# Edge items of a graph layer: ScalarE writes the gathered rows of x into the bank that the last layer adds to, and the sorting net's transpose stands last in its step

## The reference, cut to what matters

```
# x: (50000, 128)  src, dst: (12500,), dst sorted  edge_attr: (12500, 128)
edge_sum = segment_sum(edge_attr, src, num_segments=50000)
h   = elu(concatenate([x, edge_sum], axis=1) @ W0 + b0)
h   = elu(h @ W2 + b2)
out = layernorm(x + h @ W3 + b3)          # over the 128 features
```

## Time and profile before

| | |
|---|---|
| median of 3 runs | 547.99 us (544.12 to 551.29) |
| profiled execution | 546.7 us, of which span 544.9 us |
| PE busy | 507.9 us, 93% of the span |
| DVE busy | 459.7 us, 84% |
| ACT busy | 418.9 us, 77% |
| POOL busy | 371.8 us, 68% |
| mean granted TensorE clock | 0.986 of full speed |
| moved by DMA | 96.98 MB, mean 178 GB/s |

### The profile page before, as it was taken

How to read it: one execution, slowest core, us unless ns; L and a number is a source line. 1 busy time by engine, 2 the same in 40 slices (tenths; PEclk the granted TensorE clock), 3 DMA queues, 4 the chain that set the end, 5 groups by cost and what they waited for, 6 DMA issues and landing times.

```text
span 544.9 us, 10037 instructions
## 1 busy us (share of the span) xinstructions
PE 507.9 (93%) x2881; PEld 362.2 (66%) x2881; DVE 459.7 (84%) x1216; ACT 418.9 (77%) x1534; POOL 371.8 (68%) x311
## 2 busy tenths in 40 slices
PE   6898999879979999999999999999999999999980
PEld 4465656556656767777777777777777777777670
DVE  7999888878989988898898888887889888888781
ACT  4888778768877888778777777787877877877770
POOL 6877777778742787777887777777677443333355
PEclk9999999999999999999999999999999999999995
DMA  5678989888767997776666766454445443332122
GB/s 162 183 200 252 270 278 277 249 242 249 220 196 214 262 273 212 206 207 183 184 184 181 196 187 175 132 149 135 125 135 150 122 134 117 96 101 91 55 79 53
DMA packets 87756, 96.98 MB, mean 178 GB/s; under 512 B 26403, under 2 KB 56595, under 8 KB 87703
## 3 DMA queue, kind: packets, MB, share of 16 engines
q1 hardware_dynamic: 58375, 70.67, 41.5%
q0 software_dynamic: 28896, 25.29, 19.0%
q10 hardware_dynamic: 432, 0.39, 0.3%
HBM read 58.10 MB, written 45.04 MB: 189 GB/s over the span
## 4 chain that ended last, share of the span: by engine, by line
PE 72%; DMA 10%; DVE 7%; ACT 5%; issue 3%; POOLq 1%; POOL 1%; SPq 1%
PE z_ps L663 16%; PE z_ps L664 16%; PE l_ps L617 15%; PE l_ps L653 15%; DMA x_sb<-x_items_dram 7%; PE side_ps L579 4%; PE l_ps L628 4%; ACT sq L760 2%; PE side_ps L645 2%; DVE h L1025 1%; DMA words<-word_rows_dram 1%; DVE e L1023 1%; DMA word_rows_dram<-net 1%; DVE o_sb L1056 1%; POOLq L475 1%
## 5 line engine op out<-in xcount | busy, mean ns | idle before, releaser
L663 PE MATMUL z_ps<-center,xT 128*128 128x128 f32 (+1 forms) x986 | 190.4, 275 | 1.3 <-ACT xT L731 1.3
L664 PE MATMUL z_ps<-w3c,h 128*128 128x128 f32 (+1 forms) x986 | 190.1, 275 | 0.0
L663 PEld LDWEIGHTS z_ps<-center,xT 128*128 128x128 f32 (+1 forms) x986 | 154.8, 191 | 43.2 <-issue 38.7
L487 POOL DMA_INDIRECT out_dram<-pair_edge,target_i x100 | 120.9, 1209 | 89.6 <-issue 84.9
L760 ACT ACTIVATE sq<-z_ps 128x128 f32<-128x128 f32 (+1 forms) x493 | 129.3, 278 | 67.7 <-PE z_ps L664 67.2
L468 POOL DMA_INDIRECT pair_edge<-pairs_dram,edge_i x100 | 124.6, 1246 | 45.8 <-issue 30.2
L664 PEld LDWEIGHTS z_ps<-w3c,h 128*128 128x128 f32 (+1 forms) x986 | 149.0, 191 | 0.0
L458 POOL DMA_INDIRECT x_early<-in_x_dram,src_i x100 | 122.9, 1229 | 32.8 <-issue 29.6
L653 PE MATMUL l_ps<-h,w 128*128 128x512 f32 (+1 forms) x248 | 128.3, 599 | 1.0 <-DVE h L1025 1.0
L738 ACT ACTIVATE e<-l_ps,bias 128x512 f32<-128x512 f32 (+1 forms) x150 | 102.2, 682 | 21.3 <-PE l_ps L653 14.8
L1025 DVE SCALAR_TENSOR_TENSOR h<-l_ps,neg_bias,e 128x512 f32<-128x512 f32 (+1 forms) x150 | 111.1, 741 | 5.3
(11 more groups left out here) (144 smaller groups left out, 445.2 us busy)
## 6 DMA issues: line engine op xcount, KB each, us to landing
out_dram<-o_sb SPq DMA_DIRECT2D x98, 256.0 KB, 4.0
x_sb<-x_items_dram SPq DMA_DIRECT2D x97, 256.0 KB, 4.4
pairs_dram<-x_early SPq DMA_DIRECT2D x25, 250.0 KB
keyB<-key_rows_dram SPq DMA_DIRECT2D x25, 250.0 KB, 4.3
pairs_dram<-in_edge_attr_dram SPq DMA_DIRECT2D x24, 256.0 KB
x_early<-in_x_dram,src_i POOLq DMA_INDIRECT x100, 5.4
pair_edge<-pairs_dram,edge_i POOLq DMA_INDIRECT x100, 4.5
out_dram<-pair_edge,target_i POOLq DMA_INDIRECT x100
```

What stands on the lines that cost most here:

```text
L487: nc.gpsimd.indirect_dma_start(out=out[:, :], out_offset=bass.IndirectOffsetOnAxis(ap=target_i[0:EP, c:c + 1], axis=0), in_=pair_edge[0:EP ...
L663: T.matmul(z, xT[:, c % X, j * q:(j + 1) * q], center[:], start=True, stop=False)
L664: mm = T.matmul(z, h2[:, c % H, j * q:(j + 1) * q], w3c[:], start=False, stop=True)
```

## The change

For edge items the product of x with `center` goes away. Instead:

- `seed_z(c-5)`, the first part of ACT's step c, copies the four blocks of gathered rows into the four quarters of the bank `z_ps` with Identity, and takes each block's row sums (`row_sum`). It waits until the bank is free and the rows are there.
- PE waits for it (`z_seeded`), adds a row `shift_rows` (the value of `bias_x` in three bf16 parts, times ones, one bf16 matmul of 512 columns), and adds h2 times `w3c` for the four blocks.
- `take_means`, between `output` and `second_layer` on DVE, turns the row sums into two sets of negative means with two small instructions. `squares` of an edge item waits for them and uses one set as bias.
- `normalise` of an edge item becomes four instructions, (z + negative mean) times rstd, one for each block.
- The shift row is made once, in steps 35 to 37 (`split_shift`, 12 small instructions on DVE) and step 42 (a transpose, and a copy).
- A sorting step's transpose `turn_net` moves from behind `layer2` to behind `layer3`.
- In every item only the first matmul into a bank starts it (`start=j == 0`).

```
-                    T.matmul(z, xT[:, c % X, j * q:(j + 1) * q], center[:], start=True, stop=False)
-                    mm = T.matmul(z, h2[:, c % H, j * q:(j + 1) * q], w3c[:], start=False, stop=True)
+                    if ITEMS[c][0] != "edge":
+
+                        T.matmul(z, xT[:, c % X, j * q:(j + 1) * q], center[:], start=j == 0, stop=False, skip_group_check=True)
+                    mm = T.matmul(z, h2[:, c % H, j * q:(j + 1) * q], w3c[:], start=False, stop=True, skip_group_check=True)
...
+                if ITEMS[c][0] == "edge":
+
+                    pe.wait_ge(z_seeded, ITEMS[c][1] + 1)
+                    T.matmul(z_ps[c % Z][0:q, :], ones_row[0:3, 0:q], shift_rows[0:3, :, :].rearrange("p j f -> p (j f)"),
+                             start=False, stop=False, skip_group_check=True)
...
-                    beside = [lambda: None, lambda: turn_net(TURNED.index(c - SORT_AT))]
+                    beside = [lambda: None, lambda: None, lambda: turn_net(TURNED.index(c - SORT_AT))]
...
+            def seed_z(c):
+
+                g = ITEMS[c][1]
+                act.wait_ge(pair_got[g % SLOTS], got(g))
+                act.wait_ge(o_ready, c - Z + 1)
+                at_least(act, means_ready, g - 1)
+                for j in range(J):
+                    t = A.activation(z_ps[c % Z][0:EP, j * P:(j + 1) * P], pair_edge[0:EP, J * g + j, 0:P], ACT.Identity,
+                                     accum_out=row_sum[0:EP, g % 2, j:j + 1])
+                t.then_inc(z_seeded, 1)
...
+                g = ITEMS[c][1]
+                if ITEMS[c][0] == "edge":
+                    act.wait_ge(means_ready, g + 1)
                 for j in range(b):
-                    t = A.activation(sq[0:q, c % 2, j, :], z_ps[c % Z][0:q, j * P:(j + 1) * P], ACT.Square,
+                    bias = neg_mean[0:q, g % 3, 1, j:j + 1] if ITEMS[c][0] == "edge" else 0.0
+                    t = A.activation(sq[0:q, c % 2, j, :], z_ps[c % Z][0:q, j * P:(j + 1) * P], ACT.Square, bias=bias,
...
                 parts = []
+                if item_in(c - 5) and ITEMS[c - 5][0] == "edge":
+                    parts.append(lambda: seed_z(c - 5))
                 if item_in(c - 1):
...
+            def take_means(g):
+
+                dve.wait_ge(z_seeded, g + 1)
+                V.tensor_scalar(neg_mean[0:EP, g % 3, 0, :], row_sum[0:EP, g % 2, :], -1.0 / P, None, ALU.mult)
+                V.tensor_scalar(neg_mean[0:EP, g % 3, 1, :], row_sum[0:EP, g % 2, :], -float(P) ** -1.5, None, ALU.mult)\
+                    .then_inc(means_ready, 1)
...
                 elif kind == "edge":
-                    rows_out = pair_edge[0:EP, J * n:J * n + J, 0:P]
+                    for j in range(J):
+                        ins = V.tensor_scalar(pair_edge[0:EP, J * n + j, 0:P], z_ps[c % Z][0:EP, j * P:(j + 1) * P],
+                                              neg_mean[0:EP, n % 3, 0, j:j + 1], rstd[0:EP, r % 2, at + j:at + j + 1],
+                                              ALU.add, ALU.mult)
+                    ins.then_inc(o_ready, 1)
+                    return
...
+                if item_in(c - 5) and ITEMS[c - 5][0] == "edge":
+                    parts = [scale, first_layer, output, lambda: take_means(ITEMS[c - 5][1]), second_layer]
```

More of the change, by code:

```diff
@@ L115, in gnn_resnorm @@
     TURN_AT = KEY_AT + 3
+    SHIFT_AT = KEY_AT
     PAIR_X = {2 + 3 * g // 2: g for g in range(NE)}
@@ L127, in gnn_resnorm @@
     PROMPT = min(d for d in range(ND) if OUT_STEP[DENSE_AT[d]] > DENSE_AT[ND - 1 - AHEAD])
-    assert max(PAIR_X) + 4 < min(SUMS) and TURN_AT + 4 < min(SUMS)
+    assert max(PAIR_X) + 4 < min(SUMS) and TURN_AT + 5 < min(SUMS)
     assert SUM_AT[-1] > EDGE_AT[-2] - 1 and END_AT + 2 == EDGE_AT[-1] and EDGE_AT[-1] + 1 == LAST
@@ L181, in gnn_resnorm @@
         word_half = sb("word_half", [P, P], I32)
-        word_gray = sb("word_gray", [P, P], I32)
         flips = sb("flips", [P, LOG + 2, P], I32)
@@ L193, in gnn_resnorm @@
         edge_i = sb("edge_i", [P, EC], I32)
-        dup = sb("dup", [P, 3, EP])
+        dup = sb("dup", [P, 2, EP])
         target = sb("target", [P, EP])
@@ L218, in gnn_resnorm @@
         last_sum = sb("last_sum", [P, P])
+        row_sum = sb("row_sum", [P, 2, J])
+        neg_mean = sb("neg_mean", [P, 3, 2, J])
+        shift_rest = sb("shift_rest", [P, 1])
+        shift_low = sb("shift_low", [P, 1], BF16)
+        shift_parts = sb("shift_parts", [P, 3])
+        shift_rows = sb("shift_rows", [P, J, P], BF16)
         end_sumT = sb("end_sumT", [P, EC])
@@ L286, in gnn_resnorm @@
         z_ready = sem("z_ready")
+        z_seeded = sem("z_seeded")
+        means_ready = sem("means_ready")
+        shift_split = sem("shift_split")
+        shift_turned = sem("shift_turned")
+        shift_ready = sem("shift_ready")
         ssq_ready = sem("ssq_ready")
@@ L568, in turn_target, with turn_shift @@
                 T.transpose(side_ps[0:EP, 2 * P:2 * P + EC], target[0:EC, :], ident[0:EC, 0:EC]).then_inc(target_turned, 1)
+            def turn_shift():
+                pe.wait_ge(shift_split, 1)
+                pe.wait_ge(target_ready, 1)
+                T.transpose(side_ps[0:3, 0:P], shift_parts[:], ident[:]).then_inc(shift_turned, 1)
             def sums(g):
@@ L584, in sums @@
                     pe.wait_ge(target_ready, 1)
+                    pe.wait_ge(shift_ready, 1)
                 else:
@@ L699, in _ @@
                     beside = [lambda: None, lambda: None, turn_target]
+                elif c == TURN_AT + 4:
+                    beside = [lambda: None, lambda: None, turn_shift]
                 elif c in SUMS:
@@ L863, in split_b0, with split_shift, keep_shift @@
                     V.tensor_copy(bias_parts[:, part:part + 1], bias_low[:]).then_inc(parts_split, 1)
+            def split_shift(part):
+                if part == 0:
+                    link(V.tensor_copy(shift_rest[:], bias_x[:]))
+                link(V.tensor_copy(shift_low[:], shift_rest[:]))
+                if part < 2:
+                    link(V.tensor_copy(shift_parts[:, part:part + 1], shift_low[:]))
+                    link(V.tensor_tensor(shift_rest[:], shift_rest[:], shift_parts[:, part:part + 1], ALU.subtract))
+                else:
+                    V.tensor_copy(shift_parts[:, part:part + 1], shift_low[:]).then_inc(shift_split, 1)
+            def keep_shift():
+                dve.wait_ge(shift_turned, 1)
+                V.tensor_copy(shift_rows[0:3, :, :], side_ps[0:3, 0:P].rearrange("p (j f) -> p j f", j=1).to_broadcast([3, J, P]))\
+                    .then_inc(shift_ready, 1)
             def make_bias1():
@@ L886, in make_flips @@
                 for k in range(LOG):
-                    last = V.tensor_scalar(flips[:, k, :], word_gray[:], k, SIGN, ALU.logical_shift_right, ALU.logical_shift_left)
+                    last = V.tensor_scalar(flips[:, k, :], word_half[:], k, SIGN, ALU.logical_shift_right, ALU.logical_shift_left)
                 link(last)
@@ L947, in targets @@
                 V.tensor_tensor(end_dup[0:EC, :], end_before[0:EC, :], last_key, ALU.is_equal)
[L948 removed]
+                link(V.scalar_tensor_tensor(out=dup[0:EC, 0, :], in0=keyA[0:EC, :], scalar=end_before[0:EC, 0:1],
                                             in1=dup[0:EC, 1, :], op0=ALU.is_equal, op1=ALU.max))
[L950 removed]
+                V.scalar_tensor_tensor(out=target[0:EC, :], in0=dup[0:EC, 0, :], scalar=SKIP, in1=keyA[0:EC, :],
                                        op0=ALU.mult, op1=ALU.add).then_inc(target_known, 1)
@@ L1099, in _ @@
                     beside = [lambda: None, lambda: None, lambda: None, keep_target]
+                elif SHIFT_AT <= c < SHIFT_AT + 3:
+                    beside = [lambda: None, lambda: None, lambda: None, lambda: split_shift(c - SHIFT_AT)]
+                elif c == TURN_AT + 4:
+                    beside = [lambda: None, lambda: None, lambda: None, keep_shift]
                 elif c + 1 in SUMS:
```

4 lines of the change are left out of this document (1 added, 3 removed).

## The result

The changed kernel takes 583.28 us, the median of 4 runs (581.56 to 585.4), against 549.1 us for the kernel before in the same comparison. The ratio is 1.0711, with a 95% interval of 1.0666 to 1.0756: 7% slower. (The ratio leaves disturbed runs out, and stands for some 544.6 us before; the medians are over all runs.) The forecast was 574 us, with a range of 555 to 589. Its profiled execution has a span of 581.5 us, 36.6 us more than 544.9.

The account below looks back on a forecast made before the run. PE was taken as the bound at 12.67 us a group, with an equally long chain through ACT and DVE. Groups 23.1 plus end 2.4 gave 25.5 us, on the median 573.5, forecast 574 us, range 555 to 589.

Parts of the forecast that it names:

- the chain through DVE to the fourth mask: Three-step groups: ACT's squares, copies, exponential, DVE to fourth mask, PE's layer 3; 1.10 us more a group, 23.1 in 21.
- The second rival: Three-step groups: PE loses only by waiting for the seeds, 0.06 us more a group; 552 us, chance 0.10.
- PE's gain: Edge layer 3: four center matmuls go (0.88 us), one bf16 matmul comes (0.31 us); PE's work falls 0.57 us a group.
- PE's wait for the copies: Before edge layer 3: new wait of 0.32 us, or 0.93 in groups with the root ahead of the copies; mean 0.63.
- The edge squares: ACT's squares of the edge item, waiting for DVE's means: taken at 1.01 us for four.
- Both paths: Chain per group kind: 13.72 us in A (root ahead of the copies), 13.83 in B (root behind edge squares).
- The play: Groups before the change: DVE arrives with its last mask just as PE wants it, the chain as long as PE's work.
- The end: Steps 118 to 127, four edge items with no masks behind: 3.96 us more, less 1.5 hidden, 2.4 us remain.
- The cover: After the last normalise: GpSimd turns to it only at 534.19 us, which hides 1.5 us of the end's loss.
- The clock as a rival: Groups: gaps lower TensorE's clock, one layer 1 and one layer 2 at 1.2 GHz, 36 us; 610 us, chance 0.01.
- The turn and the shift: Sorting steps: moved net transpose, gain 0.6 to loss 1.8 us; split_shift in steps 35 to 37, bound 2; both taken as 0.
- the third rival: ACT in the groups: copies of 0.47 us each, 0.72 us more in each of 21 groups; 589 us, chance 0.05.

Follow-up runs that it names:

- The early masks: Changed kernel with DVE's four masks made one step earlier, in a group's first step instead of its second: 581.21 us, ratio 1.0110.
- the last run: Changed kernel with masks one step earlier, means ahead of first_layer and copies ahead of the squares of item c-6: 564.34 us, ratio 1.0381.
- The means first: Changed kernel with take_means put ahead of first_layer on DVE: 593.86 us, ratio 1.0326.

## Why the prediction was right, and where it was off

**The mechanism held.** The prediction put 23.1 of 25.5 us on the chain through DVE to the fourth mask, 13.77 us a group; it is 13.94. The early masks, which change nothing but the last link, took 1.03 us off a group. The second rival (only the wait for the seeds, 552 us) is what remains once that link is cut. As the account of the whole kernel it fell with that run. It had a group of 12.67 + 0.06 = 12.73 us, and the runs have 12.94, since PE gains less than priced (below).

**Copies.** Priced at 1.16 us for four, they take 1.19. **Means.** Priced at 0.34 us; the two take 0.13 us of DVE's time (359.07 to the next instruction at 359.20), 0.21 less than priced.

**PE's gain: a term mis-sized.** Priced at 0.57 us. The new layer 3 of the edge item runs from 356.79 to 358.09, 1.30 us, where it was 343.43 to 345.18, 1.75: 0.45. The bf16 matmul takes 0.32 until the next one (0.31 in the sum), and the four matmuls behind it (eight in the row, since each fp32 one stands twice) take 0.98 instead of 0.88. And where nothing waits, as in the group B of the last run, layer 3 starts 2.25 us into the step instead of 2.15. So 0.29 is left, 12.60 to 12.31. The sum of the groups does not use this term; the second rival and the end do.

**PE's wait for the copies.** Priced at 0.32 and 0.93 us; the rows show 0.39 and 0.91 of idle time (0.33 and 0.91 in undisturbed groups).

**The edge squares: a term mis-sized.** The chain took them at 1.01 us, like squares without a bias. Four of them with their bias take 1.38 us. The run without the operand is some 1% faster. I had read the bias as free, though the trace of before shows no Square with one and the price should have had bounds.

**Both paths held.** The sums were 13.83 for B and 13.72 for A; undisturbed groups of the kernel after take 13.93 and 14.00. The signs that the prediction named are there as well: PE idles for the copies, more and less by turns, and a second time for the last mask, 0.51 to 0.58 us in undisturbed groups, at the foot of the forecast 0.5 to 1.4. In A DVE waits for the exponential behind the edge squares (0.66 us at 459.94), 8.23 us into the group where my sum has 7.59; the bias is 0.37 of the difference. The means first took 0.77 us off A and the operand's removal 0.36. In B DVE waits for the root; 7.47 us into the group, where my sum has 6.97. That removing 0.63 and 0.37 us ahead of B's root gave only 0.30 and 0.12 is seen beside stretched DVE instructions and GpSimd's scatter issues; that these are the cause was not tested.

**The play.** Copies alone in the kernel before cost 0.27 us an undisturbed group, 0.33 over all 21. I had expected some 0.5 to 0.6. So the chain was not as tight as "arrives just as PE wants it" said. The bias, which I had left out, is of the size of that play (0.37 and some 0.3 us), and the two errors nearly cancel in the group's length, which is luck.

**The groups** came to 26.9 us for 23.1 predicted. Without the bias they come to 23.2.

**The end: the worst term.** 2.4 us predicted, 8.5 measured. The two long waits were foreseen (1.77 and 3.08 us by my sum, 1.75 and 3.06 in the rows). Three things were not.

- *The steps 118 to 123.* Put at 0.36 us, they cost 2.0 (521.27 to 549.00 in the trace after, 493.14 to 518.89 in that of before). PE waits 0.83 and 0.92 us for DVE's small parts of the last item, where it waited 0.51 at most.
- *PE's clock behind the long waits.* I had dismissed a falling clock because nothing of it showed in a stretch with 3.9 us of gaps in 40, but these single waits are longer. Against the same rows of before, the layer 2 at 553.55 takes 0.7 us more until the next matmul, the four slow rows behind it 0.7, the eight matmuls at 563.37 0.6 and the last two rows 0.5: an estimate of 2.5 us.
- *The cover.* I said that GpSimd's turn hides 1.5 us. The last scatters start 4.80 us behind PE's end, where it was 4.17, so the tail is 0.6 us longer instead of 1.5 shorter. The last normalise takes 1.36 us instead of 0.69, and GpSimd idles 4.28 us for DVE before these scatters. The edge squares' wait of 2.31 us for the means was not priced either.

These are 1.6 + 2.5 + 2.1 us, and 6.1 were missing. Which part of the change brings them is only in part shown. Without the means and the four-part normalise the end is still 8.8 us longer than before, without the copies 4.8, with the copies alone 4.5, and with early masks and the means first 5.3.

**The clock as a rival** (610 us, chance 0.01) was right to be small for the groups: 24.3 us of gaps in 278.82, none longer than 1.0, and 1.00 granted. In the end it came true, for some 2.5 us. The Trainium skill (TensorE: Matmul & The Clock Gate, HAM oscillation) warns that waits between groups of matmuls throttle the clock. The stretch with the two long waits of the end, at 0.81, agrees; the many short waits of the groups did not do it.

**The turn and the shift.** Priced at 0 with bounds of -0.6 and +1.8, and 2 us for the shift. `turn_target` starts at 175.66 us, 175.59 before. Up to step 55 1.25 us are lost, with this in the timeline of the kernel after (before, the window 170 to 182 has a clock of 1.00):

```profile
172.12 0.76 PE L687 MATMUL z_ps<-center,xT 128*128 128x128 f32 x2 [3.24 <-DVE o_sb L1126]
...
175.83 1.96 PE L634 MATMUL l_ps<-x_sb,w0x 128*128 128x512 f32 x2
```

PE reached this layer 3 early and idled for DVE; then layer 1 took 1.96 us instead of 1.02. The change is not needed for that. The kernel before with the masks earlier, which makes its first mask only at 194.58 us, has the same wait and the same slow layer 1 (its clock from 170 to 182 us is 0.72 too):

```profile
173.72 0.77 PE L663 MATMUL z_ps<-center,xT 128*128 128x128 f32 x2 [3.08 <-DVE o_sb L1056]
...
177.43 1.96 PE L617 MATMUL l_ps<-x_sb,w0x 128*128 128x512 f32 x2
```

So such a wait comes without the change, too, and the 1.25 us can't be laid on it.

**The sum.** Predicted 25.5: groups 23.1, end 2.4, rest 0. Measured 36.6: 26.9, 8.5, 1.25. The range that the sum itself gave, 568 to 583, ends just below the 583.28 measured. That the time lies well within 555 to 589 comes from the reach up to the third rival, copies of 0.47 us. They take 0.30, so what filled that room was the bias and the end: a wide margin, and not an insight.

## What to carry to other kernels

Work put on an engine that is 77% busy can still set the time: ask not how much room the engine has, but what stands behind the place where work is put in, and follow that to the next wait of the busiest engine. To find the link that holds, move one instruction of the chain without changing the work (here the masks, one step earlier). And price an operand that the trace does not show, such as a bias per row, with bounds; and look at the last items apart, where nothing covers a wait and one long wait can cost the clock too.
